# Attention softmax scaled at the output instead of at the probabilities, with new timetables

## The reference

```python
xn = _layernorm(x)
q = (xn @ Wq + bq) split in 8 heads of 128, + positions
k, v = (xn @ Wkv + bkv) halves, one head of 128; k + positions
probs = softmax(where(causal, q @ k.T / sqrt(128), min))
attn_out = (probs @ v, heads side by side) @ Wo
xr, xk = mu * xn + (1 - mu) * xn_of_the_token_before
ffn_out = sigmoid(xr @ W_r.T) * (square(relu(xk @ W_k.T)) @ W_v.T)
out = x + attn_out + ffn_out
```

## Time and profile before

| what | value |
|---|---|
| median of 3 runs | 1481.65 us (1481.39 to 1482.39) |
| the profiled execution, its own time | 1482.44 us |
| its span, first to last instruction | 1480.7 us |
| mean granted TensorE clock, share of full | 0.998 |
| instructions | 36472 |
| PE busy | 1467.7 us, 99% |
| DVE busy | 1220.7 us, 82% |
| ACT busy | 1070.8 us, 72% |
| POOL busy | 1157.3 us, 78% |
| DMA | 177.53 MB, 120 GB/s on average |

### The profile page before, as it was taken

How to read it: one execution, slowest core, us unless ns; L and a number is a source line. 1 busy time by engine, 2 the same in 40 slices (tenths; PEclk the granted TensorE clock), 3 DMA queues, 4 the chain that set the end, 5 groups by cost and what they waited for, 6 DMA issues and landing times.

```text
span 1480.7 us, 36472 instructions
## 1 busy us (share of the span) xinstructions
PE 1467.7 (99%) x11670; PEld 1440.2 (97%) x11670; DVE 1220.7 (82%) x3376; ACT 1070.8 (72%) x2569; POOL 1157.3 (78%) x1614
## 2 busy tenths in 40 slices
PE   8999999999999999999999999999999999999998
PEld 7999999999999999999999999999999999999998
DVE  6988868988688886888868898788977889778885
ACT  5777677776677767777677776777767777777774
POOL 6778877788777887778877788777887788877785
PEclk9999999999999999999999999999999999999999
DMA  4134622346224562244622455124551245512464
GB/s 129 42 107 133 201 88 68 107 140 206 80 60 114 150 189 84 63 116 146 194 73 70 117 156 187 60 70 127 173 174 48 80 131 168 181 31 77 138 189 130
DMA packets 228972, 177.53 MB, mean 120 GB/s; under 512 B 44976, under 2 KB 224176, under 8 KB 228784
## 3 DMA queue, kind: packets, MB, share of 16 engines
q1 hardware_dynamic: 227936, 174.80, 39.9%
q10 hardware_dynamic: 848, 0.40, 0.1%
HBM read 86.51 MB, written 79.17 MB: 112 GB/s over the span
## 4 chain that ended last, share of the span: by engine, by line
PE 96%; DVE 2%; POOL 1%; issue 1%; ACT 0%; DMA 0%; SPq 0%; DVEq 0%; POOLq 0%; ACTq 0%
PE pS L1108 32%; PE pO L1255 24%; PE pG L1108 16%; PE pG L1195 10%; PE pT L1211 9%; PE pS L1195 1%; PE pO L1298 1%; PE pG L1153 0%; PE pS L1153 0%; PE pO L1263 0%; POOL X L617 0%; DVE Y L988 0%; POOL pt L584 0%; DVE pt L1008 0%; DVE X L1087 0%
## 5 line engine op out<-in xcount | busy, mean ns | idle before, releaser
L1108 PE MATMUL pS<-kt,qt 128*128 128x288 f32 (+41 forms) x2304 | 462.8, 330 | 1.4 <-POOL qt L559 1.1
L825 ACT ACTIVATE X<-X,bias 128x16 f32<-128x16 f32 (+56 forms) x512 | 375.5, 734 | 70.3 <-DVE bias L1087 67.8
L617 POOL TENSOR_SCALAR X<-X,rec 128x16 f32<-128x16 f32 (+62 forms) x504 | 362.6, 719 | 53.5 <-DVE rec L978 31.2
L1108 PEld LDWEIGHTS pS<-kt,qt 128*128 128x128 f32 x2304 | 365.0, 189 | 13.0 <-issue 1.3
L584 POOL TENSOR_TENSOR pt<-pt 128x896 fp32r<-128x896 f32 (+5 forms) x184 | 325.6, 1769 | 61.5 <-ACT pt L746 59.4
L1255 PE MATMUL pO<-pt,v 128*128 128x256 f32 x2080 | 293.5, 284 | 1.1 <-DVE ot L1066 1.0
L1087 DVE CUSTOM_DVE_ANT_1 X<-pS,mask 128x528 f32<-128x528 f32 (+31 forms) x256 | 245.5, 959 | 34.5 <-PE pS L1108 26.5
L1255 PEld LDWEIGHTS pO<-pt,v 128*128 128x128 f32 x2080 | 258.7, 189 | 2.4 <-DVE ot L1066 1.4
L818 ACT CAST ot<-pO 128x256 fp32r<-128x256 f32 x256 | 95.7, 374 | 206.3 <-PE pO L1255 116.2
L1008 DVE TENSOR_TENSOR pt<-pt,pT 128x512 fp32r<-128x512 f32 (+3 forms) x432 | 203.2, 489 | 24.7 <-ACT pt L752 20.6
L752 ACT CAST pt<-pT 128x512 fp32r<-128x512 f32 (+3 forms) x440 | 186.5, 450 | 36.5 <-PE pT L1211 34.0
(11 more groups left out here) (138 smaller groups left out, 2303.9 us busy)
## 6 DMA issues: line engine op xcount, KB each, us to landing
park_dram<-Y SPq DMA_DIRECT2D x48, 448.0 KB, 3.1
pt<-park_dram SPq DMA_DIRECT2D x192, 112.0 KB, 3.0
park_dram<-Y SPq DMA_DIRECT2D x32, 512.0 KB, 3.3
pt<-park_dram SPq DMA_DIRECT2D x128, 128.0 KB, 2.8
park_dram<-Y SPq DMA_DIRECT2D x32, 384.0 KB, 3.0
pt<-park_dram SPq DMA_DIRECT2D x128, 96.0 KB, 2.4
park_dram<-Y SPq DMA_DIRECT2D x32, 320.0 KB, 2.7
pt<-park_dram SPq DMA_DIRECT2D x128, 80.0 KB, 2.2
```

Source lines behind the costliest of these rows:

```text
L617: nc.gpsimd.tensor_scalar(x_row(s, 0, w), x_row(s, 0, w), rec[:, j:j + 1], sign(s), ALU.mult, ALU.mult).then_inc(normed, 1)
L825: nc.scalar.activation(x_row(s, 0, w), x_row(s, 0, w), ACT.Exp, bias=bias[:, j:j + 1], scale=-1.0, accum_out=total[:, j:j + 1]).then_inc(e ...
L1108: last = nc.tensor.matmul(out, a[i], m[j], start=start and k == 0, stop=stop and k == n - 1)
```

## The change

- The probabilities stay unscaled. POOL only fills the padding and the copies of the last tile (`padded` takes the place of `normed`), and the sign that turned steps carried is gone.
- DVE takes the reciprocals of two steps in one instruction, once a pair, and transposes them (32x32 blocks) into `turn_rec`. A DMA, `park_rec`, writes the pair's 256 values to one row in DRAM, a second, `spread_rec`, reads that row into all 128 partitions of `rows` (3 buffers).
- DVE multiplies pO by `rows` into `rows`, which frees pO; ACT copies it out as the high part of `ot`, and POOL, no longer DVE, subtracts for the low part.
- `MODE` of row 3 loses a turned step, that of row 6 the odd step of its second pair: step 26 and step 51 are transposed by PE. Every other turned step stays, so there is still one tile of most pairs that goes by DMA.
- X has 8 halves instead of 10. No step is scaled by ACT, and the addition by DMA that no entry of `MODE` used is deleted.
- For four Q fillers in 16 (`Q_LOW`) DVE makes the low part from PSUM instead of POOL from `qtmp`. The bias of v and the copy of the turned v go from DVE to ACT.
- `T_LAG`, `PV_LAG`, `V_LAG` and `LEAD` are one less, and all tables of lags and fillers are new. In the first of them XT comes at turn 0 (before: turn 1), ahead of that turn's scores.

```diff
--- before.py
+++ after.py
-T_LAG = 6
-PV_LAG = 8
-V_LAG = 3
-F_LAG = ((5, 0), (3, 1), (4, 7), (4, 4), (4, 1), (4, 9), (5, 5), (5, 4))
-H_LAG = ((4, 6), (7, 9), (7, 6), (7, 8), (7, 6), (7, 5), (7, 7), (7, 5))
-L_LAG = ((3, 4), (3, 8), (7, 7), (7, 14), (7, 13), (7, 8), (7, 7), (7, 7))
-W_LAG = ((8, 9), (10, 7), (13, 14), (2, 3), (7, 2), (9, 2), (8, 10), (8, 14))
-MODE = ('0000', '0000', '0111', '0101', '1111', '1111', '1313', '1111')
-SCALED = (37, 43, 60)
-C_LAG = 2
+T_LAG = 5
+PV_LAG = 7
+V_LAG = 2
+F_LAG = ((5, 4), (2, 2), (4, 6), (3, 3), (5, 2), (3, 2), (4, 5), (4, 5))
+H_LAG = ((2, 6), (6, 10), (7, 6), (6, 9), (7, 7), (7, 7), (6, 6), (7, 6))
+L_LAG = ((1, 3), (2, 8), (6, 6), (6, 13), (7, 13), (7, 9), (7, 6), (6, 6))
+W_LAG = ((8, 8), (9, 6), (14, 12), (-1, -1), (7, 5), (8, 2), (6, 8), (7, 12))
+MODE = ('0000', '0000', '0111', '0001', '1111', '1111', '1113', '1111')
+PAD_LAG = 2
+REC_LAG = 2
+O_LAG = PV_LAG + 2
+PARK_AT = 3
+FETCH_AT = 5
+ROWS = 3
 QTMP = 4
-ADDED = 4
-LEAD = 11
+LEAD = 10
 PER = TPC * H
...
-WO_AT = (17, 25, 33, 41, 49, 57, 66, 73)
...
+WO_AT = (17, 25, 32, 41, 49, 57, 65, 72)
...
+Q_LOW = (3, 6, 11, 13)
...
+def low_on_dve(b, c, p):
+
+    return b is not None and 4 * (c - 1) + p in Q_LOW
...
-        X = sb("X", [P, 10, T // 2])
+        X = sb("X", [P, 8, T // 2])
         bias = sb("bias", [P, 10])
-        total = sb("total", [P, 10])
-        rec = sb("rec", [P, 10])
+        total = sb("total", [P, 4, 2])
+        rec = sb("rec", [P, 2, 32])
+        turn_rec = sb("turn_rec", [P, 2, 2, 32])
+        rows = sb("rows", [P, ROWS, 2 * P])
...
+            def park_rec(b, pair):
+
+                g = b * (STEPS // 2) + pair
+                sp.wait_ge(rec_turned, g + 1)
+                if g >= 4:
+                    sp.wait_ge(rows_landed[g % 4], 16 * (g // 4))
+                sp.dma_start(park_d[4, g % 4, 0, :].rearrange("(t q c) -> q t c", t=2, q=4),
+                             turn_rec[0:P:32, g % 2, :, :]).then_inc(rec_parked[g % 4], 16)
+
+            def spread_rec(b, pair):
+
+                g = b * (STEPS // 2) + pair
+                sp.wait_ge(rec_parked[g % 4], 16 * (g // 4 + 1))
+                if g >= ROWS:
+                    sp.wait_ge(o_lo, g - ROWS + 1)
+                sp.dma_start(rows[:, g % ROWS, :], park_d[4, g % 4, 0:1, :].broadcast_to((P, 2 * P))
+                             ).then_inc(rows_landed[g % 4], 16)
...
+                if it % 2 == FETCH_AT % 2 and 0 <= it - FETCH_AT < STEPS:
+                    spread_rec(b, (it - FETCH_AT) // 2)
                 if it - V_LAG in TURNED:
                     park(b, it - V_LAG)
+                if it % 2 == PARK_AT % 2 and 0 <= it - PARK_AT < STEPS:
+                    park_rec(b, (it - PARK_AT) // 2)
...
+                s = it - PAD_LAG
+                if 0 <= s < STEPS:
+                    w = width(s)
+                    pool.wait_ge(exp_done if packed(s) or doubled(s) else masked, b * STEPS + s + 1)
+                    pool.sem_inc(pool_passed, 1)
+                    own = (s % H + 1) * SUB
+                    if packed(s):
+                        last = x_row(s, s // H * P, (s // H + 1) * P).rearrange("p (i n) -> p i n", i=4)
+                        if own < 2 * SUB:
+                            nc.gpsimd.memset(last[:, :, own:2 * SUB], 0.0).then_inc(padded, 1)
+                        nc.gpsimd.tensor_copy(last[:, 1:4, 0:own], last[:, 0:1, 0:own].broadcast_to((P, 3, own))
+                                              ).then_inc(padded, 1)
+                    elif doubled(s):
+                        last = x_row(s, s // H * P, (s // H + 1) * P).rearrange("p (i n) -> p i n", i=2)
+                        if own < 4 * SUB:
+                            nc.gpsimd.memset(last[:, :, own:4 * SUB], 0.0).then_inc(padded, 1)
+                        nc.gpsimd.tensor_copy(last[:, 1, 0:own], last[:, 0, 0:own]).then_inc(padded, 1)
+                    elif zeroed(s):
+                        nc.gpsimd.memset(x_row(s, w, w + zeroed(s)), 0.0).then_inc(padded, 1)
...
+                    if kind == "Q" and not low_on_dve(b, c, p):
+                        split_both(b, c, p)
...
-                    pool.wait_ge(rec_ready, b * STEPS + s + 1)
...
-                    if not scaled_by_act(s):
-                        nc.gpsimd.tensor_scalar(x_row(s, 0, w), x_row(s, 0, w), rec[:, j:j + 1], sign(s),
-                                                ALU.mult, ALU.mult).then_inc(normed, 1)
...
+                first = it - O_LAG
+                if 0 <= first < STEPS and first % 2 == 0:
+                    g = b * (STEPS // 2) + first // 2
+                    pool.wait_ge(o_hi, g + 1)
+                    q0 = first % H * SUB
+                    o_out = [o[:, :, q0:q0 + 2 * SUB].rearrange("p h (t q) -> p t h q", t=2) for o in ot]
+                    nc.gpsimd.tensor_tensor(o_out[1], rows[:, g % ROWS, :].rearrange("p (t h q) -> p t h q", t=2, h=H),
+                                            o_out[0].bitcast(F), ALU.subtract).then_inc(o_lo, 1)
...
+                nc.scalar.activation(kv[:, 1, :], g[:, CHUNK:2 * CHUNK], ACT.Identity, bias=bkv[:, 1:2]).then_inc(v_sum, 1)
...
+            def value_out(b, c):
+
+                n = chunk_no(b, c)
+                act.wait_ge(filled["KT"], n + 1)
+                if b is not None:
+                    act.wait_ge(v_ready, n)
+                    act.wait_ge(v_neg, n)
+                if c == NC:
+                    act.wait_ge(kt_moved, 2 * b + 1)
+                nc.scalar.copy(kv[:, 0, :], g_bank("KT", c, 0)[:, 0:CHUNK]).then_inc(v_turned, 1)
...
-                    act.wait_ge(pv_done, b * (STEPS // 2) + pair + 1)
+                    g = b * (STEPS // 2) + pair
+                    act.wait_ge(o_scaled, g + 1)
                     q0 = first % H * SUB
                     if q0 == 0 and not (b == 0 and pair == 0):
 
                         act.wait_ge(filled["WO"], b * NT + first // H)
                     nc.scalar.copy(ot[0][:, :, q0:q0 + 2 * SUB].rearrange("p h (t q) -> p t h q", t=2),
-                                   pO[:, 0:2 * P].rearrange("p (t h q) -> p t h q", t=2, h=H)).then_inc(o_hi, 1)
+                                   rows[:, g % ROWS, :].rearrange("p (t h q) -> p t h q", t=2, h=H)).then_inc(o_hi, 1)
...
-                                         scale=-1.0, accum_out=total[:, j:j + 1]).then_inc(exp_done, 1)
+                                         scale=-1.0, accum_out=total[:, g % 4, s % 2:s % 2 + 1]).then_inc(exp_done, 1)
...
-                s = it - 2
-                if 0 <= s < STEPS:
-                    j = halves_of(s)[0]
+                first = it - O_LAG
+                if 0 <= first < STEPS and first % 2 == 0:
+                    pair = first // 2
+                    g = b * (STEPS // 2) + pair
+                    dve.wait_ge(rows_landed[g % 4], 16 * (g // 4 + 1))
+                    dve.wait_ge(pv_done, g + 1)
+                    nc.vector.tensor_tensor(rows[:, g % ROWS, :], pO[:, 0:2 * P], rows[:, g % ROWS, :], ALU.mult
+                                            ).then_inc(o_scaled, 1)
+                s = it - REC_LAG
+                if 0 <= s < STEPS and s % 2:
+                    g = pair_no(b, s)
                     dve.wait_ge(exp_done, b * STEPS + s + 1)
-                    nc.vector.reciprocal(rec[:, j:j + 1], total[:, j:j + 1]).then_inc(rec_ready, 1)
+                    if g:
+                        dve.wait_ge(rec_turned, g)
+                    else:
+                        dve.wait_ge(rec_zero, 1)
+                    nc.vector.reciprocal(rec[:, :, 0], total[:, g % 4, :]).then_inc(rec_ready, 1)
                 s = it - V_LAG
                 if s in TURNED:
                     nk = s // H + 1
                     k = turned_no(b, s)
-                    dve.wait_ge(normed, b * N_BODY + N_FIRST[s + 1])
-                    if scaled_by_act(s):
-                        dve.wait_ge(scaled, b * C_FIRST[STEPS] + C_FIRST[s + 1])
+                    dve.wait_ge(exp_done, b * STEPS + s + 1)
+                    dve.wait_ge(padded, b * N_BODY + N_FIRST[s + 1])
                     if k >= 2:
                         dve.wait_ge(parked[k % 2], 16 * (k // 2))
                     nc.vector.transpose(Y[:, k % 2, :, 0:nk, :].rearrange("p a k c -> p k a c"),
                                         x_row(s, 0, nk * P).rearrange("p (k a c) -> p k a c", a=4, c=32)
                                         ).then_inc(turned_ready, 1)
+                s = it - REC_LAG
+                if 0 <= s < STEPS and s % 2:
+                    g = pair_no(b, s)
+                    dve.wait_ge(rec_ready, g + 1)
+                    if g >= 2:
+                        dve.wait_ge(rec_parked[(g - 2) % 4], 16 * ((g - 2) // 4 + 1))
+                    nc.vector.transpose(turn_rec[:, g % 2, :, :].rearrange("p t c -> p (t c)"),
+                                        rec[:, :, :].rearrange("p t c -> p (t c)")).then_inc(rec_turned, 1)
...
```

(15 more changed lines are left out.)

185 lines of the change are left out of this document (76 added, 109 removed).

## The result

The changed kernel takes 1515.38 us (median of 4 runs, 1513.69 to 1516.43) against 1482.02 (1481.39 to 1482.90) for the kernel before: a ratio of 1.0224, 95% interval 1.0211 to 1.0237. It is 33.4 us slower. I had said slower, but by 8, and the value lies above my range of 1483 to 1500.

The account below looks back on a forecast made before the run. The prediction took PE to bound the kernel, with no idle time in the middle. Its terms, 10.6 - 2.0 - 0.5 = +8.1 us, gave a median of 1489.8 us, with a range of 1483 to 1500.

Parts of the forecast that it names:

- Transposes, +10.6: On PE: 88 more transposes, 1312 instead of 1224, cost 10.6 us, bounds 5.0 to 13.6.
- The other engines, 0 in the middle: In the middle: POOL's net -240 us, DVE's about 0 and ACT's about 27 never reach PE, so 0.
- The failed step: In the middle: PE's own stream, 2.2 us a step in rows 2 and 3, covers the other engines' work: 0.
- what would prove me wrong: Sign of a wrong prediction: PE waits in the middle for o_scaled, turned_lo or a mask.
- the tail -0.5: Tail: pO freed sooner, -0.4, WO waiting in series, +0.4, small gaps may go; taken as -0.5 us, -1.1 to +0.6.
- the start -2: Start: earlier mh and padding first in POOL's turn, against earlier XT; taken as -2 us, bounds -4 and +1.
- 1 (the start pays: Start: all idle PE and the low-clock stretch go, gaining 11.9 us, 1479.8; chance 8%, a half of it 9%.
- 2 (DVE waits for POOL's padding): Turned tiles: DVE needs padding a turn sooner and delays masks for PE, +12.7 us, 1502.4; chance 13%.
- 3 (the row comes late): Row of reciprocals: its two DMAs arrive late, 1 us in each of 8 batches, 1497.7; chance 4%.
- 4 (PE's pace by chance of order): On PE: a new timetable may gain or lose some 3 us behind transpose groups; part of the likeliest case.
- 82% for slower: Whole kernel: chance that it is slower, above the 1478.7 to 1484.6 us that counts as no change.

Follow-up runs that it names:

- e1: Kernel before with only MODE changed to the new table, so steps 26 and 51 are transposed by TensorE: 1492.18 us, ratio 1.0073.
- e6: Changed kernel with only DVE's scaling of pO moved one place earlier, ahead of the previous turn's mask: 1503.15 us, ratio 1.0142.
- e15: e6 with all low parts of q made by POOL again (Q_LOW empty): 1502.35 us, ratio 1.0137.
- e12: e1 with ACT's copy and DVE's subtraction of pO one turn later, next products unchanged: 1608.72 us, ratio 1.0857.
- e8: e6 scaling by a constant tile, without the row DMAs, output not normalized: 1500.90 us, ratio 1.0127.
- e11: e1 with the changed kernel's short lags (F_LAG but for two entries), WO turns left as they were: 1800.51 us, ratio 1.2149.
- e13: e11 with WO one turn sooner too: 1751.27 us, ratio 1.1828.
- e14: e1 with the changed kernel's timetable of fillers (TURNS and AT): 1551.15 us, ratio 1.0467.
- e7: Changed kernel scaling by a constant tile, without the row DMAs, output not normalized: 1515.04 us, ratio 1.0220.

## Why the prediction was wrong

**Transposes, +10.6: right.** e1 measured 10.6, 1312 transposes as said, 0.12 us each with what follows them. From the Trainium skill's 81 ns a matmul of 128 columns (TensorE: Matmul & The Clock Gate, Back-to-back issue gap) I had worked out 7.1 us as an estimate; the run speaks for the trace's price.

**The other engines, 0 in the middle: the load was right, the conclusion wrong.** POOL -263 us (I had -240), DVE +14 (0), ACT +20 (27). The one new form that I bounded from both sides fell outside: the transpose of 64 columns took 0.244 us, not 0.07 to 0.158. I had read the 0.947 of the earlier trace rows as the time of 896 columns, but it is the mean of six widths. None of this set the time in e6, as e15 shows for DVE's load. But I took "PE never waits in the middle" as a property of the kernel, covered by 2.2 us of PE's stream a step. It was a property of the order. I compared amounts of work with the length of a turn, and a change of order asks for another sum: for each thing that PE waits for, in which turn it is made, behind what it stands in its queue, and in which turn it is needed.

**The failed step** is the term that I put at **0** for the middle, "the cover is PE's own stream, 2.2 us a step". Between batches the changed kernel takes 4.0 us more, 28.1 in seven, and the transposes are 1.4 of each 4.0 (e1). What led me there is the sentence of the tail, "Now pO is free after one DVE operation instead of ACT's copy and DVE's subtraction", and with it the one on turns, "The steps of the batch that start one turn earlier ... shorten the pipeline only at the two ends". The first is true of the count of operations and false of the time: the operation stands a turn later behind a mask that waits for PE. From products to next products there are two turns as before, but the read of pO moved from the first to the second of them. I had looked at `o_scaled` only at the tail, and named PE's wait for it as what would prove me wrong, without working out its turn. e6 put 12.2 us on it, WO's waits included, and e12 showed that a late reader of pO alone makes both kinds of wait. I had given the tail -0.5; PE waited 1.5 us longer there. I had given the start -2; its idle time grew by 0.5.

**The rest.** 33.4 us are 10.6 for the transposes (e1), 12.2 for the scaling's place (e6), and about 11 whose cause stays open: 1503.15 against 1492.18. By the table of batches it lies in the middle: 7 x 1.59 = 11.1 us, with +1.5 at the start and -0.5 at the end. The batches of e6 are uneven, from 184.13 to 185.31 us, where e1 has 182.90 in nearly every one. In this one, 1.85 us longer than e1's, PE's records are idle for only 0.64:

```profile
565.49:750.24 184.75, 184.11 (x1466) 180.29 (x1464) 153.15 (x418) 135.88 (x329) 110.68 (x163) 1.00 0.47 133
```

The weight load is idle for 184.75 - 180.29 = 4.46 us in it, against 3.16 in e1's batch; so part of the loss may be waiting that PE's own records don't show. Some 2 us of the 11 are the row DMAs (e8); DVE's load by the q splits isn't it (e15). Left are the shorter lags and the timetable, and e11, e13 and e14 couldn't price them, as they were tuned as a set. DVE's idle time ahead of its Y transposes, which now come two turns after the scores and not three, wasn't tested either. Longer lags in the changed kernel weren't tried: as I read the code they need X halves for one more step in flight than eight give.

**The rivals.** 1 (the start pays) fell: idle time there grew. 2 (DVE waits for POOL's padding) fell as I had put it: 0.5 us against 27.1. 3 (the row comes late) fell: DVE never waited for it, and e7 without the DMAs is as slow. The row spread to 128 partitions took 3.4 us from issue to landing, 6.0 at most, with four turns to land in. The Trainium skill (DMA: Bandwidth & Descriptors, Anatomy of one DMA) gives a DMA a fixed part of about 2 us, but that section is on DMAs that GpSimd issues, and SyncE issues these; the measured time is the longer. 4 (PE's pace by chance of order) may be in the unexplained 11, as two thirds of the extra time of that batch isn't idle in PE's records; no run tests it.

**Bound and range.** 82% for slower held. The range failed because every term but PE's own work was bounded by amounts of work; I gave no chance to a wait at pO or WO.

No version here beats the kernel before: the best of the changed kind with the full computation, e15 and e6, stay 1.4% behind.

## What to carry to other kernels

When a change moves a step of a pipeline by turns, write down for every buffer the turn in which it is filled, the turn and the place in the queue at which it is read, and the turn in which it is refilled, before and after. A reader put at the start of a turn may be later than at the end of the one before, if an operation that waits for the bound engine lies between: here swapping two neighbours in DVE's queue was worth 12 us with no instruction changed. And don't price one table of a hand-tuned set by moving it alone: `WO_AT`, the lags and `TURNS` each cost 6 to 259 us by themselves, and told of the fit, not of the part.

## What was unexpected of the hardware

A DVE transpose of 64 columns took 0.244 us. The kernel before had the rows to foresee it, by width:

```profile
L988 DVE STREAM_TRANSPOSE Y<-X 128x1024 f32<-128x1024 f32 x32 | 39.7, 1239 | 14.2 <-POOL X L617 14.2
...
L988 DVE STREAM_TRANSPOSE Y<-X 128x384 f32<-128x384 f32 x24 | 13.6, 566 | 3.1 <-POOL X L617 3.1
```

From 384 to 1024 columns it took 0.673 us more, 1.05 ns a column; carried on to 64 columns that leaves 0.16 us that doesn't depend on the width and gives 0.23, an estimate from these two rows.

HBM reads were 80.75 MB without the 256 broadcasts of one row to 128 partitions (e7) and 114.30 with them. The 33.55 MB between are 256 times 128 KB: every partition's copy is read from HBM anew. The changed kernel's time didn't notice (e7).
